# Four transformer blocks on one core: the third bf16 part of queries and keys is copied by POOL's queue instead of SyncE's, and eleven start-up loads are issued at another place

## The chip, the cores and the metric

One core of a Trainium2 chip runs the whole program. The time is device microseconds from launch to end, the median of several runs. The program has the five engines' instruction streams: TensorE (PE), VectorE (DVE), ScalarE (ACT), GpSimd (POOL) and SyncE (SP), each in order. DMAs are started by SP's, ScalarE's and POOL's queues.

## The reference

The input is 16 sequences of 256 tokens with 256 features, and for each a context of 77 tokens. Four layers follow each other:

```python
# layer 0: pre-norm decoder block
x = x + mha(ln1(x), ln1(x), causal) @ m_proj_w + m_proj_b
x = x + mha(ln2(x), ctx)            @ c_proj_w + c_proj_b
x = x + relu(ln3(x) @ f_w1 + f_b1) @ f_w2 + f_b2
# layer 1: post-norm, with a mixture of experts
x = ln1(x + attn(x, x, causal));  x = ln2(x + attn(x, ctx))
p = softmax(x @ router_w + router_b); two best of 8 experts, softmax over the two
x = ln3(x + sum over the two of weight * (gelu(x @ w1[e] + b1[e]) @ w2[e] + b2[e]))
# layer 2: post-norm with a given mask;  layer 3: one more cross attention
x = ln1(x + mha(x, x, mask)); x = ln2(x + mha(x, ctx)); x = ln3(x + relu(x @ w1) @ w2)
x = ln(x + attn(x, ctx) @ Wo)
```

Every attention has 16 heads of 16 features. So there are three self attentions (numbered 0, 2, 4) and four cross attentions (1, 3, 5, 6) per sequence. All data are float32.

## The kernel before

**Three phases.** Phase a runs layer 0 and layer 1 up to the router for all 16 sequences and scatters each token's row to the rows of its two experts. Phase b runs the experts in 39 groups of 256 rows. Phase c gathers the results and runs the rest. The span of the profile divides into a to some 1560 us, b to some 2125 us, and c.

**The plan.** In phases a and c the work of one sequence is a chain of small steps, each on one engine; up to six sequences are in flight. Before anything is emitted, a planner (`Plan.run`) places all steps by costs written beside them (`us`, and `lag` until a result is usable) and gives each engine one fixed list. Among steps that can start at the same time it takes the more urgent one; urgency is the length of the way that is left, plus a lead from the table `AHEAD` (line 437) by stage of the work (`enters`, `norms`, `projs`, `shifts`, `gains`, `outs` and others) and by attention. At run time an engine works through its list in order and waits on semaphores.

**Stacks.** The scores need nearly float32 accuracy from bf16 matmuls. So queries and keys are cut into three bf16 parts: `high` (ScalarE, line 916), `rest` (DVE, 1071), `middle` (ScalarE, 921), `low` (POOL, 1288), in a tile `parts` of 128 partitions. Six blocks of 16 partitions then form a stack (`qs`, `ks`, or `ctx_ks` for the context's keys), in which each part stands once or several times, so that one matmul over 96 rows gives the product. `COPIES` says which: the first part is copied to three blocks, the second to two, the third to one, for each role. Each copy is a DMA from SBUF to SBUF, issued by SP (line 1343), 128 KB, or 38.5 KB for the context's keys. Each part's copies wait for the step that makes the part, and stand in SP's list in the order of the parts. The scores by query (`qm`, line 702, with a mask matmul at 835 or 839) wait for the last copies of both roles.

**Shifts.** DVE takes the maxima of the scores (1081), cuts them in three parts (to line 1100), PE turns them (710), ScalarE copies them to `shift` (925), and SP writes them below the query stack by a DMA (1346). Only then do the scores by key (`km`, 722) and the exponentials (932) follow, then probabilities times values (738), further turns (748, 757) and the output projection (774).

**Other users of the queues.** SP also issues the inputs (1328), the context (1331), the start-up loads (1325) and the stores. POOL does the eps and power steps of the norms (1268, 1273), gains and biases (1280, 1284, 1294), and the indirect scatters and gathers (1308, 1299); in phase b it issues the weights of phase c by plain DMAs (1312).

**Start-up loads.** Groups of constants have a queue and a step behind which they are issued (`LOADS`, line 412). The group `rows` has 14 loads: three bias rows, four gain and shift rows of the norms l1_1 and l1_2, the router and its bias, and five of tables and masks. SP issues them right behind the input of the third sequence.

Of the kernel before, what the change touches and what calls it, by code (L numbers as in the profile page):

```python
# [14 lines left out]
P = 128  # L15
B, S, D = 16, 256, 256
H, HD = 16, 16
# [250 lines left out]
def parts_steps(plan, b, at, role, xt, source, after=(), gives=()):  # L268
# [14 lines left out]
    order = [("copy", b, at, (role, part)) for part in range(NPART)]  # L283
    for part, kind in enumerate(("high", "middle", "low")):
        plan.step("sync", "copy", b, at, (role, part), us=0.63 * len(COPIES[role == "q"][part]), lag={"q": 4.6, "k": 5.6, "c": 2.4}[role],
                  after=[(kind, b, at, role)], behind=order[part - 1:part], gives=["parts"] if part == NPART - 1 else [],
                  landing="stack", transfers=len(COPIES[role == "q"][part]), stack=stack, parts=parts)
    return stack
# [91 lines left out]
def self_attention(plan, b, at, xt, turned):  # L380
# [3 lines left out]
    stacked = [("copy", b, at, (role, part)) for role in "qk" for part in range(NPART)]  # L384
# [3 lines left out]
def cross_attention(plan, b, at, xt, turned, context):  # L388
    qs = parts_steps(plan, b, at, "q", xt, turned, gives=["xt"])
    ks, values = context  # L390
    stacked = [("copy", b, at, (role, part)) for role in "qc" for part in range(NPART)]
# [3 lines left out]
def feed_forward(plan, b, at, xt, turned, residual, with_bias):  # L395
    hidden = ("qs", (b, at))
    for f in range(FT // 2):
# [15 lines left out]
         "bias": ("scalar", None), 1: ("sync", ("enter", 1, "a")), "rows": ("sync", ("enter", 2, "a")),  # L413
# [3 lines left out]
def start_steps(plan, loads):  # L417
    plan.pool("weights", len(LOADS))
    for name, (queue, step) in LOADS.items():
# [5 lines left out]
    plan.step("vector", "fold", -1, "a", us=0.4, after=[("load", -1, "a", "rows")])  # L425
# [11 lines left out]
AHEAD = {"a": {("shifts", 0): 0.1, ("shifts", 1): 2.4, "ends": 0.3, "enters": -1.1, "ffs": 8.0, ("gains", 2): 7.6,  # L437
               "norms": 0.6, ("norms", 3): 3.7, ("norms", "l0_ff"): -0.3, "outs": -0.7, ("outs", 1): 0.3,
               ("outs", 2): 0.6, "projs": 0.8, ("projs", 1): -0.2, "pvs": -1.0, "scores": 0.1, "turns": -0.6,
               ("turns", 1): 3.1, "values": -0.4, ("values", 0): 2.4},  # L440
         "c": {"shifts": 0.8, "ends": 0.1, ("ends", 4): -0.3, "enters": 2.2, "ffs": -0.7, ("ffs", 6): 0.5,
               ("maxima", 5): -0.2, "gains": -4.3, ("norms", 5): 1.2, ("outs", 6): 0.2, "projs": 0.2, "pvs": -0.1,
               "scores": 1.7, ("scores", 6): -0.3, "turns": 0.1, ("turns", 6): 0.1, ("turns", "l2_ff"): -0.4,
# [873 lines left out]
def sync_program(sp, k, phase):  # L1317
# [3 lines left out]
    for s in k.plan.order[phase]["sync"]:  # L1321
# [10 lines left out]
        elif s.kind == "copy":  # L1332
# [5 lines left out]
            elif part == 1:  # L1338
                until.wait_ge(*done("middle", b, at, role))
            else:  # L1340
                until.wait_ge(*done("low", b, at, role))
# [363 lines left out]
```

## Time and profile before

| | us |
|---|---|
| median of 3 runs | 3290.51 (3286.32 to 3300.18) |
| the profiled execution | 3307.31 |
| its span, first to last instruction | 3305.5 |
| PE busy | 3046.6 (92%) |
| DVE busy | 1561.7 (47%) |
| ACT busy | 1541.9 (47%) |
| POOL busy | 872.2 (26%) |
| mean granted clock of PE | 0.960 |

The shares are of the span. DMA issues are not counted as busy on SP's queue, so SP has no row. A wait is put down to what released it. "PEclk" is the granted clock, as a share of full speed. The page counts these stack copies of 128 KB on SP: 384 and 288 for queries, 192 and 96 for keys, in the first and second half, and 192 and 192 of 38.5 KB for the context's keys.

### The profile page before, as it was taken

Reading aid. Unit: us, or ns where it says so; the run is one execution under the profiler, and the core shown is the slowest. Engines: PE = TensorE matmul, PEld = TensorE weight load, DVE = VectorE, ACT = ScalarE, POOL = GpSimd, SP = SyncE. Lnnn points to the kernel's source line nnn. Section 1 sums busy time; section 2 is a strip of 40 time slices with the busy share of each in tenths; the row PEclk is TensorE's granted clock in tenths of the full one; section 3 lists DMA queues with packets and bytes.
Section 4 is the critical chain, followed back from the end, with each engine's and each line's share of the span. In section 5 each row is a group of like instructions: output and inputs, shape, how many; then the busy total and the mean of one; then the engine's idle time right before and its main releaser. Section 6 shows DMA issues by size and latency. Waiting matters only on the chain. (4 is left out here: it accounts for less than half of the span.)

```text
span 3305.5 us, 61810 instructions
## 1 busy us (share of the span) xinstructions
PE 3046.6 (92%) x23959; PEld 2472.7 (75%) x24016; DVE 1561.7 (47%) x4057; ACT 1541.9 (47%) x3403; POOL 872.2 (26%) x991
## 2 busy tenths in 40 slices
PE   7999999899999999885999999789999999999996
PEld 5788877678876777764888888656777777777774
DVE  4644465554466556444101110166555566565542
ACT  3555556455555555452222222145455555555652
POOL 2121234222133322322000000142243444334331
PEclk8999999899999999997999999899999999999997
DMA  9734345463355553743766665365255546444431
GB/s 167 98 53 62 55 69 90 69 91 45 55 78 88 83 74 53 172 62 97 242 218 221 199 198 197 104 107 65 33 73 68 81 69 82 63 71 78 62 49 24
DMA packets 394607, 319.34 MB, mean 97 GB/s; under 512 B 151711, under 2 KB 378271, under 8 KB 394303
## 3 DMA queue, kind: packets, MB, share of 16 engines
q1 hardware_dynamic: 371062, 276.77, 46.8%
q0 software_dynamic: 8272, 23.73, 2.8%
q10 hardware_dynamic: 14981, 14.89, 1.6%
q8 instruction: 190, 3.11, 0.5%
q14 instruction: 102, 0.84, 0.1%
HBM read 134.33 MB, written 37.22 MB: 52 GB/s over the span
## 5 line engine op out<-in xcount | busy, mean ns | idle before, releaser
L1081 DVE TENSOR_REDUCE a_maxima<-a_bank 128x2 f32<-128x512 f32 (+3 forms) x576 | 339.8, 646 | 177.1 <-PE a_bank L702 173.3
L932 ACT ACTIVATE a_prob<-a_bank 128x512 f32<-128x512 f32 (+1 forms) x640 | 338.8, 600 | 138.0 <-PE a_bank L722 134.0
L1081 DVE TENSOR_REDUCE c_maxima<-c_bank 128x2 f32<-128x512 f32 (+2 forms) x448 | 259.1, 636 | 178.5 <-PE c_bank L702 178.3
L932 ACT ACTIVATE c_prob<-c_bank 128x512 f32<-128x512 f32 (+1 forms) x512 | 264.4, 599 | 150.9 <-PE c_bank L722 150.2
L968 ACT ACTIVATE b_group_hidden<-b_bank,b_b 128x256 f32<-128x256 f32 x312 | 131.0, 471 | 421.4 <-PE b_bank L790 421.4
L835 PE MATMUL a_bank<-a_causal_b,keep_identb 128*128 128x256 bf16 (+1 forms) x768 | 248.0, 323 | 57.0 <-DMA a_qs<-a_shift 38.2
L790 PE MATMUL b_bank<-b_group_xt,b_w 128*128 128x256 f32 x1248 | 284.1, 381 | 0.8 <-DVE b_group_xt L1122 0.8
L774 PE MATMUL b_bank<-b_w,b_group_hidden 128*128 128x256 f32 x1248 | 275.8, 379 | 0.9 <-ACT b_group_hidden L968 0.9
L774 PEld LDWEIGHTS b_bank<-b_w,b_group_hidden 128*128 128x128 f32 x1248 | 237.0, 190 | 33.5 <-ACT b_group_hidden L968 1.3
L790 PEld LDWEIGHTS b_bank<-b_group_xt,b_w 128*128 128x128 f32 x1248 | 235.5, 191 | 31.9 <-DVE b_group_xt L1122 1.2
L1127 DVE TENSOR_TENSOR b_group_y<-b_bank,b_b 128x512 f32<-128x512 f32 x39 | 27.0, 691 | 364.4 <-PE b_bank L774 364.4
L1118 DVE TENSOR_TENSOR a_tok<-a_bank,a_tok 128x512 f32<-128x512 f32 x80 | 55.2, 690 | 205.3 <-PE a_bank L774 198.3
L722 PE MATMUL a_bank<-a_qs,a_ks 99*128 99x128 bf16 x1536 | 149.0, 226 | 0.5 <-issue 0.5
L722 PEld LDWEIGHTS a_bank<-a_qs,a_ks 99*128 99x128 bf16 x1536 | 125.6, 102 | 25.0 <-issue 3.8
L702 PE MATMUL a_bank<-a_ks,a_qs 96*128 96x128 bf16 x1536 | 144.0, 223 | 0.0
L943 ACT ACTIVATE a_raw<-a_bank 128x512 f32<-128x512 f32 x128 | 76.4, 597 | 138.7 <-PE a_bank L738 124.7
L702 PEld LDWEIGHTS a_bank<-a_ks,a_qs 96*128 96x128 bf16 x1536 | 122.3, 100 | 24.3 <-issue 2.2
L680 PE MATMUL a_bank<-a_xt,a_at_q 128*128 128x256 f32 x512 | 133.7, 407 | 4.9 <-ACT a_xt L905 2.3
L1288 POOL TENSOR_TENSOR a_parts_q<-a_rest,a_parts_q 128x512 bf16<-128x512 f32 x64 | 74.3, 1160 | 225.3 <-ACT a_parts_q L921 225.2
L774 PE MATMUL a_bank<-a_at_o,a_heads 128*128 128x256 f32 x512 | 128.2, 395 | 5.8 <-ACT a_heads L949 5.7
L835 PEld LDWEIGHTS a_bank<-a_causal_b,keep_identb 128*128 128x128 bf16 x768 | 77.6, 101 | 73.2 <-DMA a_qs<-a_shift 42.0
L1280 POOL TENSOR_TENSOR c_tok<-c_tok,weights_row_L_xattn_ln_g 128x512 f32<-128x512 f32 x64 | 81.6, 1275 | 162.6 <-PE c_bank L671 162.4
(239 smaller groups left out, 6542.4 us busy)
## 6 DMA issues: line engine op xcount, KB each, us to landing
b_w<-in_L_xattn_e_w SPq DMA_DIRECT2D x78, 1024.0 KB, 7.3
a_qs<-a_parts_q SPq DMA_DIRECT2D x384, 128.0 KB
c_qs<-c_parts_q SPq DMA_DIRECT2D x288, 128.0 KB
a_ks<-a_parts_k SPq DMA_DIRECT2D x192, 128.0 KB
c_ks<-c_parts_k SPq DMA_DIRECT2D x96, 128.0 KB
b_group_x<-sorted_in SPq DMA_DIRECT2D x39, 256.0 KB, 6.8
sorted_out<-b_group_y ACTq DMA_DIRECT2D x39, 256.0 KB, 5.2
sorted_in<-a_zeros SPq DMA_DIRECT2D x8, 1024.0 KB
```

What stands on the lines that cost most here:

```text
L680: ins = pe.matmul(bank[:, 0, m * n:(m + 1) * n], weight[:, kt, m * P:(m + 1) * P], xt[:, kt, 0:n], start=(kt == 0), stop=(kt == KT - 1))
L702: ins = pe.matmul(bank[:, 0, to:to + m], qs[0:STACK, h, q * P:(q + 1) * P], ks[0:STACK, h, kt * P:kt * P + m], start=(at in CROSS), stop=( ...
L722: ins = pe.matmul(bank[0:kn, 0, to:to + m], ks[0:STACK + NPART, h, kt * P:kt * P + kn], qs[0:STACK + NPART, h, q0:q0 + m], start=(at in CR ...
L774: ins = pe.matmul(bank[:, 0, q * D:(q + 1) * D], heads[:, kt, q * P:(q + 1) * P], weight[:, kt, :], start=(kt == 0), stop=(kt == kts - 1))
L790: ins = pe.matmul(bank[:, 0, j * S:(j + 1) * S], weight[:, kt, f * P:(f + 1) * P], xt[:, kt, :], start=(kt == 0), stop=(kt == KT - 1))
L835: pe.matmul(blocks, k.identb, k.causal[:, keys_first, :].unsqueeze(1).broadcast_to([P, 4 // step, P]), start=True, stop=False)
L932: act.activation(prob[0:rows, first:first + cols], bank[0:rows, 0, 0:cols], ACT.Exp, scale=SCALE).then_inc(k.own(s), 1)
L943: act.activation(tile(s, "raw"), tile(s, "bank")[:, 0, :], ACT.Copy).then_inc(k.own(s), 1)
L968: ins = act.activation(hidden[:, f, :], bank[:, 0, j * S:(j + 1) * S], ACT.Gelu, bias=b1[:, f:f + 1])
L1081: v.tensor_reduce(maxima[:, q:q + qn, h:h + n].rearrange("p q h -> p h q"), bank[:, 0, 0:cols].rearrange("p (j q n) -> p j q n", j=n, q=qn ...
L1280: pool.tensor_tensor(x, x, over(k.gains[at][0]), ALU.mult).then_inc(k.own(s), 1)
L1288: pool.tensor_tensor(parts[:, 2, :, 0:n], rest[:, :, 0:n], parts[:, 1, :, 0:n], ALU.subtract).then_inc(k.own(s), 1)
```

## The change

The third part's copy becomes a step of POOL, `low_copy`, issued after POOL's own `low` step; SP keeps the copies of the first two parts. PE waits for both. The `high` step, which writes into a `parts` tile, waits for the earlier user's second and third copies. The planner counts 1.0 us of POOL for the new step, where it had 0.63 us of SP, and the same lag. The group `rows` is split: three bias rows stay, and the other eleven loads form the group `gains`, behind the shift DMA of sequence 0's second attention. The table of leads gets other values for both phases, so the order of all engines' lists differs.

```diff
--- before.py
+++ after.py
@@ parts_steps
-    order = [("copy", b, at, (role, part)) for part in range(NPART)]
-    for part, kind in enumerate(("high", "middle", "low")):
-        plan.step("sync", "copy", b, at, (role, part), us=0.63 * len(COPIES[role == "q"][part]), lag={"q": 4.6, "k": 5.6, "c": 2.4}[role],
-                  after=[(kind, b, at, role)], behind=order[part - 1:part], gives=["parts"] if part == NPART - 1 else [],
+    lag = {"q": 4.6, "k": 5.6, "c": 2.4}[role]
+    for part, kind in enumerate(("high", "middle")):
+        plan.step("sync", "copy", b, at, (role, part), us=0.63 * len(COPIES[role == "q"][part]), lag=lag,
+                  after=[(kind, b, at, role)], behind=[("copy", b, at, (role, 0))] if part else [],
                   landing="stack", transfers=len(COPIES[role == "q"][part]), stack=stack, parts=parts)
+    plan.step("gpsimd", "low_copy", b, at, role, us=1.0, lag=lag, after=[("low", b, at, role)],
+              behind=[("copy", b, at, (role, 1))], gives=["parts"], landing="stack", stack=stack, parts=parts)
@@ LOADS
-         "bias": ("scalar", None), 1: ("sync", ("enter", 1, "a")), "rows": ("sync", ("enter", 2, "a")),
+         "bias": ("scalar", None), 1: ("sync", ("enter", 1, "a")), "rows": ("sync", ("enter", 2, "a")), "gains": ("sync", ("shift_in", 0, 1)),
@@ AHEAD
-AHEAD = {"a": {("shifts", 0): 0.1, ("shifts", 1): 2.4, "ends": 0.3, "enters": -1.1, "ffs": 8.0, ("gains", 2): 7.6,
-               "norms": 0.6, ("norms", 3): 3.7, ("norms", "l0_ff"): -0.3, "outs": -0.7, ("outs", 1): 0.3,
-               ("outs", 2): 0.6, "projs": 0.8, ("projs", 1): -0.2, "pvs": -1.0, "scores": 0.1, "turns": -0.6,
-               ("turns", 1): 3.1, "values": -0.4, ("values", 0): 2.4},
-         "c": {"shifts": 0.8, "ends": 0.1, ("ends", 4): -0.3, "enters": 2.2, "ffs": -0.7, ("ffs", 6): 0.5,
-               ("maxima", 5): -0.2, "gains": -4.3, ("norms", 5): 1.2, ("outs", 6): 0.2, "projs": 0.2, "pvs": -0.1,
-               "scores": 1.7, ("scores", 6): -0.3, "turns": 0.1, ("turns", 6): 0.1, ("turns", "l2_ff"): -0.4,
+AHEAD = {"a": {("shifts", 0): 0.1, ("shifts", 1): 2.4, "ends": 0.3, "enters": 1.1, "ffs": 8.0, ("maxima", 0): -0.2,
+               "gains": -0.5, ("gains", 2): 7.6, ("gains", "l0_ff"): -3.9, "norms": 1.2, ("norms", 0): -1.1,
+               ("norms", 3): 3.7, ("norms", "l0_ff"): -0.8, "outs": -0.7, ("outs", 1): 2.2, ("outs", 2): 1.0,
+               "projs": 0.8, ("projs", 1): -0.2, "pvs": -1.0, ("pvs", 1): 0.1, ("pvs", "l0_ff"): -0.2, "scores": 0.1,
+               "turns": -0.6, ("turns", 1): 3.1, "values": -0.3, ("values", 0): 2.4},
+         "c": {"shifts": 0.8, ("shifts", 6): 1.1, "ends": 0.1, ("ends", 4): -0.4, "enters": 0.6, ("enters", 4): -1.0,
+               ("enters", 6): 0.2, "ffs": -0.7, ("ffs", 6): 0.5, ("maxima", 5): -0.2, "gains": -2.1, "norms": -0.1,
+               ("norms", 4): -0.2, ("norms", 5): 1.2, "outs": -0.3, ("outs", 4): -0.3, ("outs", 5): 2.3,
+               ("outs", 6): 0.2, ("outs", "l2_ff"): 3.0, "projs": 0.2, "pvs": -0.1, "scores": 1.7, ("scores", 4): 0.3,
+               ("scores", 5): -0.1, ("scores", 6): -0.3, "turns": 0.1, ("turns", 6): -0.1, ("turns", "l2_ff"): -0.4,
                ("values", 5): 2.0}}
@@ tensor_program, qm
-            until.wait_ge(*done("copy", b, at, ("q", NPART - 1)))
-            until.wait_ge(*done("copy", b, at, ("k" if at in SELF else "c", NPART - 1)))
+            for role in "qk" if at in SELF else "qc":
+                until.wait_ge(*done("copy", b, at, (role, 1)))
+                until.wait_ge(*done("low_copy", b, at, role))
@@ scalar_program, high
-            until.wait_ge(*freed(s, "parts"))
+            earlier = k.plan.earlier[s.tiles["parts"]]
+            if earlier:
+                until.wait_ge(*done(*earlier))
+                until.wait_ge(*done("copy", earlier[1], earlier[2], (earlier[3], 1)))
@@ gpsimd_program
+        elif s.kind == "low_copy":
+            stack, (block,) = tile(s, "stack"), COPIES[s.part == "q"][NPART - 1]
+            until.wait_ge(*done("low", b, at, s.part))
+            until.wait_ge(*freed(s, "stack"))
+            pool.dma_start(stack[block * HD:(block + 1) * HD, :, :],
+                           tile(s, "parts")[:, NPART - 1, :, 0:C if s.part == "c" else S]).then_inc(k.own(s), 16)
@@ sync_program, copy
-            elif part == 1:
+            else:
                 until.wait_ge(*done("middle", b, at, role))
-            else:
-                until.wait_ge(*done("low", b, at, role))
...
```

The steps that waited for the load `rows` and need one of the moved constants (the fold of a bias into a shift row, the router's matmul, the table steps) wait for `gains` instead.

## Rows read from the trace of the kernel before

**Rows 1.** The page: the engines' busy us and shares; DVE's maxima, mean ns of one.

```profile
PE 3046.6 (92%) x23959; PEld 2472.7 (75%) x24016; DVE 1561.7 (47%) x4057; ACT 1541.9 (47%) x3403; POOL 872.2 (26%) x991
...
L1081 DVE TENSOR_REDUCE a_maxima<-a_bank 128x2 f32<-128x512 f32 (+3 forms) x576 | 339.8, 646 | 177.1 <-PE a_bank L702 173.3
```

**Rows 2.** Windows: us; busy us (count) of PE, PEld, DVE, ACT, POOL; PEclk, DMA share, GB/s.

```profile
100.00:1400.00 1300.00, 1219.06 (x11265) 1002.23 (x11263) 712.37 (x1959) 695.55 (x1523) 358.37 (x403) 0.97 0.51 76
...
1400.00:1562.00 162.00, 103.97 (x994) 82.15 (x994) 70.91 (x226) 64.21 (x134) 40.74 (x44) 0.81 0.37 74
...
2181.00:3200.00 1019.00, 986.44 (x7847) 759.65 (x7902) 608.30 (x1471) 563.76 (x1242) 362.93 (x407) 0.99 0.48 67
...
3200.00:3306.00 106.00, 73.29 (x468) 54.15 (x466) 32.80 (x94) 32.03 (x70) 23.83 (x28) 0.78 0.18 31
```

**Rows 3.** Waits of PE: line, releaser, us in total, times, longest.

```profile
PE a_bank L835 <- DMA a_qs<-a_shift: 38.2, 12, 9.1
...
PE c_bank L722 <- DMA c_qs<-c_shift: 29.8, 13, 7.2
...
PE a_bank L722 <- DMA a_qs<-a_shift: 7.2, 3, 3.7
...
PE a_bank L835 <- DMA a_qs<-a_parts_q: 6.0, 3, 4.2
```

**Rows 4.** Windows around the wait of PE at 600 us.

```profile
590.00:608.00 18.00, 8.19 (x83) 6.87 (x82) 13.59 (x42) 5.42 (x13) 6.04 (x5) 0.79 1.12 142
608.00:615.00 7.00, 7.00 (x56) 5.70 (x57) 0.00 (x0) 3.78 (x7) 0.00 (x0) 0.57 0.16 22
```

**Rows 5.** The chain that ended last, at 2873 and 3273: start, us, what.

```profile
2873.61 7.96 DMA c_qs<-c_shift
...
3273.19 2.72 DMA c_qs<-c_shift
```

**Rows 6.** Timeline of SP's queue and ScalarE before that shift: start, us, what.

```profile
2872.31 0.61 SPq L1343 DMA_DIRECT2D c_ks<-c_parts_k  x1
...
2872.96 0.61 SPq L1343 DMA_DIRECT2D c_qs<-c_parts_q  x1
...
2873.61 0.75 SPq L1346 DMA_DIRECT2D c_qs<-c_shift  x1
...
2872.79 0.38 ACT L925 ACTIVATE c_shift<-c_bank 48x256 bf16<-48x256 f32 x1 [1.37 <-PE c_bank L710]
```

**Rows 7.** Window of the burst ahead of it.

```profile
2868.00:2875.00 7.00, 7.00 (x63) 5.53 (x57) 5.88 (x14) 5.10 (x13) 4.56 (x6) 1.00 1.14 124
```

**Rows 8.** Groups of POOL's DMAs: count, busy us, mean ns, idle before.

```profile
L1308 POOL DMA_INDIRECT sorted_in<-a_tok,keep_rows x64 | 63.8, 997 | 87.4 <-DVE keep_rows L1206 65.1 <-issue 15.5 <-DMA x_moe_in<-a_tok 6.9
...
L1312 POOL DMA_DIRECT2D weights_row_L_xattn_ln_g<-in_rows x4 | 2.2, 545 | 54.4 <-DMA b_group_x<-sorted_in 54.4
...
L1312 POOL DMA_DIRECT2D c_weights_at_v<-in_L_xattn_ca_wv x1 | 0.7, 712 | 13.4 <-DMA b_group_x<-sorted_in 13.4
```

**Rows 9.** Lines 1308 and 1312 (last row): duration ns and landing, min/median/max.

```profile
L1308 POOL DMA_INDIRECT sorted_in<-a_tok,keep_rows x64: 959/963/1227, 473.5 to 1547.3; - x64
...
DMA to landing us min/median/max: 6.4/7.5/8.8
...
DMA to landing us min/median/max: 3.2/3.4/9.2
```

**Rows 10.** Timeline of SP's queue and PE at the start.

```profile
16.41 0.43 SPq L1325 DMA_DIRECT2D a_row_L_xattn_ln_g<-in_rows  x1
...
21.39 1.97 SPq L1343 DMA_DIRECT2D a_ks<-a_parts_k  x3
...
34.80 0.59 PE L835 MATMUL a_bank<-a_causal_b,keep_identb 128*128 128x512 bf16 x1 [4.18 <-DMA a_qs<-a_parts_q]
```

**Rows 11.** Waits of SP's queue for POOL, the largest.

```profile
SPq L1343 <- POOL c_parts_q L1288: 18.2, 11, 2.0
```

**Rows 12.** Timeline of PE: the first scores that read the stack of rows 6.

```profile
2885.34 0.38 PE L702 MATMUL c_bank<-c_ks,c_qs 96*128 96x256 bf16 x2
```

More of the change, by code:

```diff
@@ L383, in self_attention @@
     values = value_steps(plan, b, at, "v", xt, turned, after=[("proj", b, at, "k")], gives=["xt"])
-    stacked = [("copy", b, at, (role, part)) for role in "qk" for part in range(NPART)]
+    stacked = [(kind, b, at, part) for role in "qk" for kind, part in (("copy", (role, 1)), ("low_copy", role))]
     return attend_steps(plan, b, at, qs, ks, values, stacked)
@@ L390, in cross_attention @@
     ks, values = context
-    stacked = [("copy", b, at, (role, part)) for role in "qc" for part in range(NPART)]
+    stacked = [(kind, b, at, part) for role in "qc" for kind, part in (("copy", (role, 1)), ("low_copy", role))]
     return attend_steps(plan, b, at, qs, ks, values, stacked)
@@ L424, in start_steps @@
     plan.step("vector", "cast", -1, "a", us=1.0, after=[("load", -1, "a", "first"), ("load", -1, "a", "masks")])
-    plan.step("vector", "fold", -1, "a", us=0.4, after=[("load", -1, "a", "rows")])
+    plan.step("vector", "fold", -1, "a", us=0.4, after=[("load", -1, "a", "gains")])
 STAGES = {"enters": ("enter", "ctx_load"), "norms": ("stats", "moments", "eps", "rstd", "apply"), "turns": ("turn", "turned"),
@@ L507, in route_steps @@
     r = ("route", b)
-    plan.step("tensor", "route", b, "a", us=0.86, source=turned, after=[("load", -1, "a", "rows")], takes=["bank", "r"], gives=["xt"],
+    plan.step("tensor", "route", b, "a", us=0.86, source=turned, after=[("load", -1, "a", "gains")], takes=["bank", "r"], gives=["xt"],
               xt=xt, bank=bank, r=r)
@@ L814, in tensor_program @@
             xt = tile(s, "xt")
-            until.wait_ge(*done("load", -1, "a", "rows"))
+            until.wait_ge(*done("load", -1, "a", "gains"))
             until.wait_ge(*done(*s.source))
@@ L1006, in vector_program @@
         elif s.kind == "fold":
-            until.wait_ge(*(done("load", -1, "a", "rows") if at == "a" else k.c_loaded))
+            until.wait_ge(*(done("load", -1, "a", "gains") if at == "a" else k.c_loaded))
             for shift, bias in k.folds[at]:
@@ L1222, in table_step @@
     until.wait_ge(*(k.done("table", s.b, "a", s.part - 1) if s.part else k.done("run", s.b, "a")))
-    until.wait_ge(*k.done("load", -1, "a", "rows"))
+    until.wait_ge(*k.done("load", -1, "a", "gains"))
     if s.part == 0:
@@ L1539, in build_phases @@
         k.out_bias["l0_ff"] = row(c, n0("f_b2"))
+        c.group = "gains"
         k.gains["l1_1"], k.gains["l1_2"] = [(row(c, n1(f"ln{i}_g")), row(c, n1(f"ln{i}_b"))) for i in (1, 2)]
@@ L1567, in build_phases @@
                             (k.run[:, 0, :], a["regions"].partition_broadcast(P))]
-        c.loads["rows"] += [(k.table["steps"], a["steps"].partition_broadcast(P)),
+        c.loads["gains"] += [(k.table["steps"], a["steps"].partition_broadcast(P)),
                             (k.table["upto"].rearrange("p a b -> p (a b)"), a["upto"].partition_broadcast(1)),
```

## The prediction

> **What bounds the kernel now.** I read four views, in this order. The page gives TensorE (PE) 92% of the span [rows 1], so the first question is what the other 8% is and not which engine to relieve. The windows by stage [rows 2] place it. From 100 to 1400 us (first half, steady) PE is busy 1219 of 1300 us: 81 us idle, and its granted clock averages 0.97. While the first half drains (1400 to 1562) it is busy 104 of 162 us. In the steady second half 986 of 1019, in its tail 73 of 106. The expert stage between them runs full and has no step of this change. So the second half can give some 33 us steady and 33 in the tail, and the first half 81 and 58, plus what the clock loses.
>
> The waits of PE by releaser [rows 3] say who ends that idle time. The largest releaser in either half is a DMA that SP's queue issued: the row shifts into the query stack (38.2, 7.2 and 29.8 us) and, small, the query parts into the stack (6.0). Together 81.2 us in 31 waits. A long one costs more than its length: after the wait of 7.7 us at 600 the clock is 0.57 over the next 7 us, the lower of its two levels (1.2 of 2.4 GHz) for most of it, 3.0 us of work lost [rows 4].
>
> The fourth view is the chain around one such wait. The shift DMA issued at 2873.61 is the longest link, 7.96 us, where one with nothing in front of it takes 2.72 us at 3273.19 [rows 5]. ScalarE had the shift ready at 2872.79 + 0.38 = 2873.17; SP still issued two third parts, 0.61 us each, so 0.44 us went by in SP's queue [rows 6]. The other 7.96 - 2.72 = 5.2 us are spent behind earlier transfers: 16 DMA engines are 1.14 busy from 2868 to 2875 and move 124 GB/s [rows 7], or 128 KB in 1.06 us, while SP issues one each 0.65 us. So in a burst the transfers, more than the issuing, set when the shift lands.
>
> **The change part by part.** *Copies moved.* One copy per role and attention: per sequence 8 in the first half, 6 in the second, times 16 = 224 of 1344; 64 of them are of the short context keys. SP loses 224 x 0.61 = 137 us of issuing, spread over 2700 us. Most of it buys nothing, as SP sits idle between bursts. It counts where a shift DMA stands behind them. SP's waits for POOL's low step vanish too: the largest group is 18.2 us in 11 [rows 11], and the queued copies behind it (those of the next part or the shift) become free.
>
> What one wait gains, from both sides: nothing, if the shared engines are the limit; at most two issues (1.2 us) plus one sixth of the 5.2 us backlog (0.9), if the third parts leave the ring that the shift queues in and are served in the gaps: 2.1 us. At the row read closely only 0.4 of the issue time was usable, and I give half of the ring's share, because POOL's copies want the same engines at the same time: 0.4 + 0.5 = 0.9 us. Without the start's wait (below) 30 waits are left, so 27 us. Clock: the long wait has 3.0 us lost beside 7.7, short ones nothing at 0.99 mean [rows 2, 4]; I take a factor 1.2, which is 32 us. PE's order is fixed, so part of it is handed to the next wait; no other releaser comes near in total, so I keep two thirds: **-21 us** (bounds 0 and 30 x 2.1 x 1.4 = -88).
>
> The Trainium skill (DMA: Bandwidth & Descriptors, Issuing engines are not separate DMA queues) says that DMAs of several issuing engines end up on the same 16 engines and that spreading the issue saves only the issuer's time. The 1.14 busy share of [rows 7] agrees. By that rule alone the 0.5 us of ring share is nothing, and the term would be 30 x 0.4 x 1.2 x 2/3 = -10 us. It is the second rival below.
>
> *POOL's added work.* The trace has no stack copy from POOL. The nearest are its direct loads: 0.54 us for 128 KB of rows and 0.71 for 256 KB of weights; an indirect one takes 1.00 us, with some 0.3 us between two [rows 8]. I price the 160 long copies as the former and the 64 short as the latter, plus 0.3 each: 86 + 46 + 67 = 199 us (upper bound by the indirect rows, 224 x 1.3 = 290; lower bound without gaps 132). POOL goes from 363 busy of 1019 us in the second half [rows 2] to some 450. What stands behind a copy on POOL: the eps and rstd steps of the norms, gains, biases, gathers and scatters. A norm step meets an issue in some 8% of cases (199 us of 2700), for half an issue, and PE then waits for DVE's apply step; over 160 norms that is 160 x 0.08 x 0.45 = 6 us on a chain that is mostly hidden under five other sequences. **+2 us** (0 to +8). If that cover were gone it would be the 6 us, twice in places where POOL also has gathers.
>
> *Landing of the third part.* The scores start only with every part in place. On SP the last third part was issued at 2872.96 and the scores that read it began at 2885.34 [rows 6, 12], 12.4 us later. POOL's direct loads land 3.4 us after the issue in the median, 9.2 at worst, its scatters 7.5 [rows 9]. Even 9.2 plus two 1.3 us elementwise steps ahead of it fits into 12.4. Cost 0 where the slack is like this; rival three prices where it isn't. The `high` step's wait for a free parts buffer now names both copies; the same events, no cost.
>
> *An issue held up by DVE.* 64 scatters, issued on POOL beside a DVE that is busy over half of the time [rows 2], take 959/963/1227 ns at the least, middle and most [rows 9]: held up by 0.27 us at most. Cost 0; rival four is the other case. The Trainium skill (SBUF — State Buffer, the trap "DVE blocks DMA") says that DVE instructions in certain modes keep GpSimd from writing the descriptors of its DMAs, 620 ns becoming 3100; the trace disagrees so far.
>
> *The constants.* Fourteen loads are issued behind the third sequence's input at the start. By the diff three stay (`rows`) and eleven (`gains`) go behind a shift DMA of sequence 0's second attention. Eleven issues stand from 16.41 to 21.39, 5.0 us, and the first copy into a stack comes right after, at 21.39; PE's first scores wait 4.18 us for those copies and start at 34.80 [rows 10]. With the copies 5 us earlier this wait goes: **-4 us** (0 to -6; sequence fill has later waits that can take it back). The eleven come back as 5 us of SP's queue in the middle of sequence 0's copies, once: **+2 us** (0 to +5).
>
> *The order.* The planner's leads are changed for 13 entries and more, enters, norms, outs, gains above all, in both halves; every engine's list comes out different. No row prices that. The 81 idle us of 100 to 1400 are single waits with no period, so a new order deals them anew: 0, with +-15.
>
> Sum: -21 + 2 - 4 + 2 = -21 us. The profiled execution took 3307.31 us (span 3305.5); with the change 3286. It is 16.8 us above the median of the timed runs, 3290.5; the same step from there gives **3269.5 us**, -0.64%.
>
> **The rivals.** *One, the new order is itself better.* Leads that fit the queues close waits that no copy causes, a third of the steady 81 + 33 us and of the clock's 39 (1300 x 0.03): some 50 us, 3240. For it: the large first-half waits are irregular. Against: it needs most of them to close together.
>
> *Two, it hides anyway.* The DMA engines set the landing, SP's freed time is idle time; the start gives 2 to 4 and the rest is noise: 3290.5 - 3 = 3287. For it: [rows 7], and that the landing stays at 8 us however the copies are split. Against: [rows 6] has the shift behind two of the very copies that move.
>
> *Three, the third part becomes the late one.* It waits in POOL's order behind elementwise steps, then needs 7.5 us like a scatter instead of some 3.4. Its place is the first scores matmul of an attention; it decides from where less than about 10 us lie between issue and scores. If that is so for one in four of the 112 attentions, with 1.3 us each and the clock's 1.2: 28 x 1.3 x 1.2 = 44 us, less 9 of what the forecast gains: 3325. For it: query parts already end three waits of PE [rows 3]; waits of POOL's own kind at the drain, where nothing covers. Against: the slack of 12.4 us.
>
> *Four, DVE holds up POOL's issues.* An issue that has to wait for a DVE instruction of 0.65 us, the mean of its maxima [rows 1], costs up to that each time: 224 x 0.65 = 146 us more on POOL, which then issues for 345 us; a norm step meets that in 13% of cases for 0.8 us, 160 x 0.13 x 0.8 = 17 us, and with third parts 0.65 us later the forecast's gain is gone beside it: -21 + 17 + 2 = 3288. Against: the scatters' 0.27 us. The skill's SBUF rule above is this rival.
>
> **How the numbers follow.** Forecast 0.42; rival one 0.12; two 0.25; three 0.18; four 0.03. About 0.5% (16 us) is what a measurement tells from no change, so faster means under 3274. The forecast with its +-15 falls there for 0.36 of its 0.42 when its size is right, but its size is uncertain by half, so 0.31; rival one gives 0.12, rival two 0.05: faster 0.48. Slower (over 3307): 0.17 from three, 0.03 from two, 0.01 from the forecast: 0.21. Same 0.31. Range: rival one and most of three inside, 3230 to 3315.
>
> **What would show it.** Right: PE's waits for the two shift DMAs fall from 75 to about 50 us in sum; the first scores start near 30.6 instead of 34.80; POOL-issued stack copies at 0.5 to 0.7 us; mean clock of 100 to 1400 rises. Wrong: the shift's link stays near 8 us (rival two), PE waits for `low_copy` transfers by name (rival three), or issues on POOL over 1.3 us (the rule on DVE).

## The result, and the profile after

The changed kernel takes **3342.51 us** (median of 4 runs, 3332.84 to 3345.05); the kernel before, measured beside it, 3289.94 (4 runs, 3286.32 to 3300.18). The ratio is **1.0148** (95% interval 1.0123 to 1.0174): 1.5% slower, where 0.64% faster was forecast. The profiled executions took 3345.05 and 3307.31 us.

The page after, first part and DMA queues (packets, MB, share of 16 engines):

```profile
PE 3051.1 (91%) x23951; PEld 2479.2 (74%) x24016; DVE 1554.1 (46%) x4057; ACT 1547.6 (46%) x3403; POOL 1008.4 (30%) x1215
...
q1 hardware_dynamic: 330614, 253.26, 42.5%
q0 software_dynamic: 18000, 47.24, 8.0%
```

The queues before:

```profile
q1 hardware_dynamic: 371062, 276.77, 46.8%
q0 software_dynamic: 8272, 23.73, 2.8%
```

TensorE does the same work. POOL has 1008.4 - 872.2 = 136 us more, the moved copies and no more. Their 23.5 MB have gone from q1 to q0. The two queues together take 50.5% of the engines' time where they took 49.6%; in e1 below, with the same order and every copy on SP, they take 50.6%, so the larger share need not come from the issuer (columns as above):

```profile
q1 hardware_dynamic: 371062, 276.77, 47.8%
q0 software_dynamic: 8272, 23.73, 2.8%
```

The windows that answer to [rows 2], and PE's waits that answer to [rows 3]:

```profile
100.00:1400.00 1300.00, 1209.39 (x11271) 1000.58 (x11268) 711.85 (x1960) 696.66 (x1521) 422.85 (x512) 0.97 0.54 78
1400.00:1562.00 162.00, 110.33 (x1009) 87.54 (x1010) 69.11 (x222) 65.84 (x138) 43.95 (x50) 0.79 0.35 84
2181.00:3200.00 1019.00, 956.31 (x7503) 734.31 (x7564) 579.06 (x1415) 544.10 (x1193) 393.99 (x467) 0.97 0.47 63
```

```profile
PE c_bank L728 <- DMA c_qs<-c_shift: 58.7, 12, 7.2
PE a_bank L841 <- DMA a_qs<-a_shift: 58.2, 14, 18.8
PE a_bank L728 <- DMA a_qs<-a_shift: 12.8, 7, 3.8
...
PE a_bank L841 <- DMA a_ks<-a_parts_k: 6.1, 2, 5.2
...
PE a_bank L708 <- DMA a_ctx_ks<-a_parts_k: 2.3, 2, 1.2
PE a_bank L841 <- DMA a_qs<-a_parts_q: 1.8, 1, 1.8
```

Lines 841, 728 and 708 are 835, 722 and 702 of before. In the steady second half PE is busy for 30 us less (986.44 to 956.31), and its clock is two hundredths lower; its wait for the shift has doubled (29.8 to 58.7). The same releaser as before ends these waits, so no new wait appeared: the old one grew. The next table divides the time by phase. A half ends with PE's last instruction of it; the second half is counted from the end of the expert phase, which takes some 561 us in each. "Low clock" is the time at which PE's granted clock stood at 1.2 GHz and not 2.4.

| profile | first scores at | first half ends | second half lasts | low clock in the second half |
|---|---|---|---|---|
| before | 34.8 | 1542.3 | 1172.0 | 92.6 |
| before, a second profile | 35.2 | 1540.1 | 1171.3 | 89.0 |
| after | 31.8 | 1530.5 | 1218.8 | 157.0 |

**All of the loss is in the second half: +47 us.** The first half of this trace ends 10 to 12 us earlier, but two other kernels with the same first half (below) end it at 1542.6 and 1547.2, so that is no gain to rely on. Of the 47 us, PE's idle time makes up 28.5 (82.3 to 110.8 in the second half), which is the growth of the one wait for the shift (28.9). The low clock lasted 64 us longer, and at half speed that costs 32. Together this is 14 us more than the loss; what gave those back is open.

The chain of waits after, its links of this kind in the second half (start, us, what; "..." marks rows left out):

```profile
2748.31 8.59 DMA c_qs<-c_shift
...
2821.81 9.68 DMA c_qs<-c_shift
2831.54 2.78 PE c_bank L728 x12
...
2895.33 8.29 DMA c_qs<-c_shift
...
2967.35 9.83 DMA c_qs<-c_shift
...
3309.36 2.74 DMA c_qs<-c_shift
```

Against [rows 5] the link behind a burst of copies has grown, from 7.96 us to between 8.3 and 9.8; the one with nothing ahead of it has not. It recurs once per sequence. SP's queue around it shows what changed (first after, then the row of before that follows the shift of [rows 6]):

```profile
2878.90 6.42 SPq L1356 DMA_DIRECT2D c_qs<-c_parts_q  x8
2885.37 3.22 SPq L1356 DMA_DIRECT2D c_ks<-c_parts_k  x5
2888.63 1.26 SPq L1356 DMA_DIRECT2D c_qs<-c_parts_q  x2
2890.37 4.27 SPq L1356 DMA_DIRECT2D c_ctx_ks<-c_parts_k  x5
2895.33 0.76 SPq L1359 DMA_DIRECT2D c_qs<-c_shift  x1
```

```profile
2874.46 4.84 SPq L1343 DMA_DIRECT2D c_ctx_ks<-c_parts_k  x6
```

Before, the context's key copies of the next attention stood behind the shift of attention 5. After, five of them stand ahead of it, though SP has fewer copies in all: the planner has put them there.

PE and the clock around the wait at 2825 us, and the windows over it (columns as in [rows 2]):

```profile
2823.76 1.89 PE L796 MATMUL c_bank<-c_xt,c_weights_f 128*128 128x256 f32 x8
2831.54 2.78 PE L728 MATMUL c_bank<-c_qs,c_ctx_ks 99*77 99x256 bf16 x12 [5.89 <-DMA c_qs<-c_shift]
```

```profile
2824.00:2832.00 8.00, 2.11 (x11) 1.53 (x10) 0.00 (x0) 2.41 (x6) 2.18 (x2) 0.87 0.77 50
2832.00:2836.00 4.00, 3.78 (x17) 2.83 (x17) 0.69 (x1) 3.12 (x6) 0.00 (x0) 0.50 0.00 0
```

After 5.9 us without work PE runs at least 4 us at half clock.

### The profile page after: what moved, and what is told of

Read it like the earlier page. It is cut to its first block and busy times, and to the rows that moved or that the text cites. A ratio compares the mean times of both kernels' runs of the same rounds, so it can differ in the third digit from the quotient of the medians.

```text
span 3343.1 us, 62041 instructions
## 1 busy us (share of the span) xinstructions
PE 3051.1 (91%) x23951; PEld 2479.2 (74%) x24016; DVE 1554.1 (46%) x4057; ACT 1547.6 (46%) x3403; POOL 1008.4 (30%) x1215
## 5 line engine op out<-in xcount | busy, mean ns | idle before, releaser
L1090 DVE TENSOR_REDUCE a_maxima<-a_bank 128x2 f32<-128x512 f32 (+2 forms) x576 | 339.2, 647 | 140.2 <-PE a_bank L708 139.6
L841 PE MATMUL a_bank<-a_causal_b,keep_identb 128*128 128x256 bf16 (+1 forms) x768 | 245.5, 320 | 73.4 <-DMA a_qs<-a_shift 58.2
L728 PE MATMUL c_bank<-c_qs,c_ctx_ks 99*77 99x256 bf16 x512 | 85.8, 315 | 61.0 <-DMA c_qs<-c_shift 58.7
L1297 POOL TENSOR_TENSOR c_parts_q<-c_rest,c_parts_q 128x512 bf16<-128x512 f32 x48 | 55.6, 1158 | 255.4 <-ACT c_parts_q L930 255.4
L685 PE MATMUL a_bank<-a_xt,a_at_q 128*128 128x256 f32 x512 | 127.0, 392 | 4.4 <-ACT a_xt L911 2.3
```

The costliest lines, as they stand in the source:

```text
L685: ins = pe.matmul(bank[:, 0, m * n:(m + 1) * n], weight[:, kt, m * P:(m + 1) * P], xt[:, kt, 0:n], start=(kt == 0), stop=(kt == KT - 1))
L728: ins = pe.matmul(bank[0:kn, 0, to:to + m], ks[0:STACK + NPART, h, kt * P:kt * P + kn], qs[0:STACK + NPART, h, q0:q0 + m], start=(at in CR ...
L841: pe.matmul(blocks, k.identb, k.causal[:, keys_first, :].unsqueeze(1).broadcast_to([P, 4 // step, P]), start=True, stop=False)
L1090: v.tensor_reduce(maxima[:, q:q + qn, h:h + n].rearrange("p q h -> p h q"), bank[:, 0, 0:cols].rearrange("p (j q n) -> p j q n", j=n, q=qn ...
L1297: pool.tensor_tensor(parts[:, 2, :, 0:n], rest[:, :, 0:n], parts[:, 1, :, 0:n], ALU.subtract).then_inc(k.own(s), 1)
```

## The experiments

Between 2300 and 3200 us PE waits for the shift of attention 5 once per sequence, ten times in most kernels (the count is given where it differs). Each such wait divides exactly. *Queue* is the time from the shift being ready on ScalarE to the issue of its DMA. *Issue to go* runs from that issue to the first scores by key. *PE work* is what PE still had to do once the shift was ready. Then queue + issue to go - PE work = wait. The table gives means per wait, the sum of all of them, and how long the second half lasts, in us.

| kernel | queue | issue to go | PE work | wait | sum of waits | second half |
|---|---|---|---|---|---|---|
| before | 0.62 | 7.48 | 6.34 | 1.76 | 17.6 | 1172.0 |
| after | 0.29 | 9.27 | 4.73 | 4.82 | 48.2 | 1218.8 |
| e1, SP issues all | 1.72 | 8.30 | 4.73 | 5.29 | 52.9 | 1223.7 |
| e2, POOL issues, old lists (9 waits) | 0.02 | 7.93 | 6.37 | 1.59 | 14.3 | 1179.0 |
| e3, old leads in the second half (6) | 0.47 | 9.15 | 5.30 | 4.32 | 25.9 | 1222.5 |
| e4, before, shift on ScalarE (9) | 0.03 | 7.69 | 6.28 | 1.44 | 12.9 | 1162.3 |
| e5, after, shift on ScalarE | 0.03 | 9.58 | 4.77 | 4.84 | 48.4 | 1220.0 |
| f1, after, shift first | 0.03 | 7.54 | 4.73 | 2.83 | 28.3 | 1189.4 |
| f4, before, context first | 4.26 | 5.99 | 6.33 | 3.92 | 39.2 | 1207.9 |
| g2, before, new leads | 0.67 | 8.36 | 5.11 | 3.92 | 39.2 | 1217.1 |

The expectations name four theories. R: third copies on POOL's queue hold up the shift. O: the new leads leave PE too little work between a shift and the scores by key. Neither outlived e1 to e3, and P and L took their place. P: the planner puts copies ahead of the shift in SP's list. L: what matters is PE's own list. All ratios are to the kernel before on the same chip (median 3312 to 3319 there, 22 to 29 us above that of the main comparison), with the 95% interval. "..." in a diff marks lines left out.

**Third copies back on SP, everything else as after** (each third copy is put into SP's list at its planned time):

```diff
+        began = lambda s: self.began[s.kind, s.b, s.at, s.part]
+        order["sync"] = sorted(order["sync"] + [s for s in order["gpsimd"] if s.kind == "low_copy"], key=began)
+        order["gpsimd"] = [s for s in order["gpsimd"] if s.kind != "low_copy"]
...
```

> The changed kernel with the lists of PE, DVE, ACT and POOL as they are, but the third copies issued by SP, at the time where the planner put them; POOL only loses them. Theory R (the third copies on POOL's ring hold up the shift DMA and make the second half slower): the wait of PE for the c_qs shift, 58.7 us in the changed kernel, falls back to about 30 us and the time to about 3290 to 3300 us. Theory O (the new leads' order of the second half leaves too little PE work between a shift and the scores by key): the wait stays at 50 to 75 us and the time at 3335 to 3355 us.

Measured: 3357.59 us, 1.0134 (1.0107 to 1.0161), as slow as the changed kernel: theory R fails.

```profile
PE c_bank L733 <- DMA c_qs<-c_shift: 63.8, 13, 7.2
```

Who issues the third parts matters little in the second half (1223.7 us against 1218.8); the lists do.

**Third copies on POOL, the lists of before** (each right behind its `low` step):

```diff
+            third = {(s.b, s.at, s.part[0]): s for s in order["sync"] if s.kind == "copy" and s.part[1] == NPART - 1}
+            order["sync"] = [s for s in order["sync"] if not (s.kind == "copy" and s.part[1] == NPART - 1)]
+            order["gpsimd"] = [x for s in order["gpsimd"] for x in
+                               ([s, third[s.b, s.at, s.part]] if s.kind == "low" else [s])]
...
```

> The kernel before with all its lists, but the third copies issued by POOL, each right behind the low step. Theory R: the second half grows by about 50 us as in the changed kernel, the time is 3330 to 3345 us. Theory O: the copies' mover is harmless or a small gain, 3275 to 3300 us, the wait for the c_qs shift 20 to 35 us.

Measured: 3331.55, 1.0053 (1.0034 to 1.0072); first half to 1557.9, second half 1179.0. The time lies in R's range, but not for R's reason: that was to be some 50 us in the second half, which grew by 7, and the wait for the shift is as O had it.

```profile
PE c_bank L729 <- DMA c_qs<-c_shift: 26.5, 12, 8.1
PE c_bank L677 <- DVE c_tok L1073: 17.3, 11, 4.9
```

The move alone costs 0.5%, a third of the loss, and most of that in the first half. It shortens the queue term from 0.62 to 0.02 us, lengthens issue to go by 0.45, and leaves the wait about where it was. The second row is PE's wait for DVE's step of a norm, which itself stands behind POOL's eps and power steps. It was 7.4 us in 3 waits before (10.7 in the second profile of that kernel): part of what the move costs in the second half goes through the norms.

**After, with the old leads in the second half** (the `"c"` table of `AHEAD` from before):

> The changed kernel with the leads of the kernel before in the second half only (first half and POOL's copies as changed). Theory O: the second half goes back to its 1172 us or some 10 more, and with the first half 12 us shorter as in the changed kernel's profile the time is 3275 to 3295 us. Theory R: the second half stays at 1210 to 1225 us, the time at 3330 to 3350 us.

Measured: 3356.49, 1.0116 (1.0073 to 1.0159); second half 1222.5, against O's 1172 to 1182. Theory O fails: the old leads do not bring the time back once the planner charges the third copy to POOL.

```profile
PE c_bank L726 <- DMA c_qs<-c_shift: 39.0, 9, 7.1
...
PE c_bank L714 <- DVE c_least_parts L1107: 10.5, 5, 2.7
...
PE c_bank L706 <- DMA c_ks<-c_parts_k: 9.2, 2, 7.9
```

The shift waits are not the whole story here. They grew by 9 us (29.8 to 39.0), while all idle time of PE in the second half grew by 32 (82.3 to 114.2). The rest is spread over others: the last piece of the maxima (the L714 row; 2.6 us before), a key copy, DVE's norm step (14.3, 7.4 before).

**Before, with the new leads** (both tables of `AHEAD` from after, all copies on SP):

> The kernel before with the changed kernel's two tables of leads, third copies on SP and counted there. By the lists that come out, in 6 sequences of the second half the shift DMA of attention 5 has no context copy in the run of copies ahead of it, in others 3 to 6. If it is the leads that put the context copies ahead of the shift, the second half is 1210 to 1225 us; if it takes the planner's counting of the third copies on POOL as well, it is 1170 to 1195 us, the time 0.998 to 1.008 of the kernel before.

Measured: 3372.5, 1.0178 (1.0155 to 1.0201); second half 1217.1, first half to 1560.0.

```profile
PE c_bank L725 <- DMA c_qs<-c_shift: 49.6, 12, 7.2
```

The new leads alone, with no copy on POOL and no load moved, cost as much as the whole change in the second half (+45 us), and 18 us more in the first. In the six last of the ten sequences no context copy stands in the burst ahead of the shift. The wait grows through less PE work between the shift and the scores by key (6.34 to 5.11) and a later landing (7.48 to 8.36). So context copies ahead of the shift are one way to lose this time, and not the only one: e3 and g2 each have one half of the new plan, and each loses as much as both halves together.

**Before, context copies ahead of the shift.** Nothing else is altered: in 8 sequences the six copies of attention 6's context keys change places with the shift of attention 5.

```diff
+            line = order["sync"]
+            for i in range(len(line) - 1, -1, -1):
+                s = line[i]
+                if s.kind == "shift_in" and s.at == 5:
+                    j = i
+                    while j + 1 < len(line) and line[j + 1].kind == "copy" and line[j + 1].at == 6 and line[j + 1].part[0] == "c":
+                        line[j], line[j + 1] = line[j + 1], line[j]
+                        j += 1
```

> The kernel before with the reverse: in SP's list of the second half the six context-key copies of attention 6 that stand behind the shift DMA of attention 5 (8 sequences) stand ahead of it. Theory P: each of the 8 shifts lands about 2.5 us later, or with SP's 6 x 0.65 us of issuing up to 4; PE's wait for the c_qs shift rises from 30 to 50 to 60 us, the second half by 20 to 45 us; the time is 1.006 to 1.014 of the kernel before. Theory L: within 0.3% of the kernel before.

Measured: 3354.79, 1.0128 (1.0104 to 1.0153); second half +36 us, as P expected.

```profile
PE c_bank L731 <- DMA c_qs<-c_shift: 49.7, 12, 7.2
```

```profile
2892.21 5.05 SPq L1352 DMA_DIRECT2D c_ctx_ks<-c_parts_k  x6
2897.30 0.75 SPq L1355 DMA_DIRECT2D c_qs<-c_shift  x1
```

Six small copies in front of the shift reproduce most of the loss. They do it by another term than in the changed kernel, though: here SP's queue grows (0.62 to 4.26 us) and issue to go shrinks (7.48 to 5.99), while in the changed kernel SP has issued the copies before the shift is ready, and issue to go grows (to 9.27).

**After, the shift ahead of those copies** (11 sequences), the opposite edit:

```diff
+            line = order["sync"]
+            for i, s in enumerate(line):
+                if s.kind == "shift_in" and s.at == 5:
+                    j = i
+                    while line[j - 1].kind == "copy" and line[j - 1].at == 6 and line[j - 1].part[0] == "c":
+                        line[j], line[j - 1] = line[j - 1], line[j]
+                        j -= 1
```

> The changed kernel with one change in SP's list of the second half: where the shift DMA of attention 5 stands behind context-key copies of attention 6 (one to five transfers, 11 sequences), it now stands ahead of them. Nothing else moves. Theory P (the planner, which counts a copy at its issuing queue only, filled the time freed on SP with those copies ahead of the shift, and it lands about 2.5 us later): PE's wait for the c_qs shift falls from 58.7 to 25 to 40 us, and with the lower clock behind waits of 4 to 6 us the second half gets 20 to 40 us shorter; the time is 0.6 to 1.2% below the changed kernel, so 1.003 to 1.009 of the kernel before. Theory L (it is the work that PE has between the shift and the scores, set by PE's list): the wait stays over 50 us, the time within 0.3% of the changed kernel's.

Measured: 3327.63, 1.0036 (1.0023 to 1.0050), as P expected and not L; second half 1189.4, 29 us of the 47 recovered.

```profile
PE c_bank L736 <- DMA c_qs<-c_shift: 38.7, 12, 7.2
```

Issue to go returns to that of before (9.27 to 7.54). The missing PE work (4.73) stays, and so does a wait 1.1 us longer than before; this is the likely, untested, cause of the 17 us that are left of the loss.

**The shift issued by ScalarE**, right behind the instruction that makes it, in before:

```diff
+            shifts = {(s.b, s.at): s for s in order["sync"] if s.kind == "shift_in"}
+            order["sync"] = [s for s in order["sync"] if s.kind != "shift_in"]
+            order["scalar"] = [x for s in order["scalar"] for x in
+                               ([s, shifts[s.b, s.at]] if s.kind == "turned_shift" else [s])]
...
```

> The kernel before, with the shift DMA issued from ScalarE's queue right behind the step that makes the shift, not from SP's; everything else, lists included, as before. If the backlog of SP's ring is what makes a shift land after 8 us and not 2.7, it lands after 3 to 5 us, most of PE's 75 us of waits for it go, and the time is 3240 to 3265 us. If the 16 shared engines set the landing whatever the ring, it stays near 8 us and the time at 3285 to 3295 us.

Measured: **3265.11, 0.9855 (0.9827 to 0.9884)**; first half to 1510.4, second half 1162.3.

```profile
PE c_bank L727 <- DMA c_qs<-c_shift: 21.8, 12, 5.0
PE a_bank L840 <- DMA a_qs<-a_shift: 15.8, 5, 5.8
PE a_bank L727 <- DMA a_qs<-a_shift: 2.8, 2, 1.9
```

and the same edit in after:

> The changed kernel with the shift DMA issued from ScalarE's queue, right behind the step that makes it. It no longer stands behind SP's copies and the clearing DMAs (18.8 us wait at 1385 us), but shares the 16 engines with all that was issued before. Theory P: most of what the change lost comes back, since what stands ahead in SP's list no longer matters for the issue: about 0.988 to 0.998 of the kernel before, as the same step took 1.45% from the kernel before. If the loss is in PE's list, 1.003 to 1.010 is left.

Measured: 3315.8, 1.0011 (0.9996 to 1.0027); first half to 1504.8, second half still 1220.0. P had expected 0.988 to 0.998 and misses; the result lies between that and the 1.003 to 1.010 of a loss in PE's list. The copies ahead of the shift delay it whichever queue issues it.

```profile
PE c_bank L733 <- DMA c_qs<-c_shift: 56.6, 12, 5.9
```

The own queue takes away the whole queue term and nothing of issue to go, which is 7.69 us in e4 (7.48 before) and 9.58 in e5 (9.27 after). So e4's expectation came out by halves: the landing as if the shared engines set it, the time as if it had become short. Most of the gain, 32 of the 40 us by which e4's trace is shorter, is in the first half, where SP's queue held some shifts back for long. In the changed kernel one shift was ready at 1380.49 and could go only behind this row of clearing stores,

```profile
1369.39 23.46 SPq L1369 DMA_DIRECT2D sorted_in<-a_zeros  x9
```

which gave PE its longest wait for a shift, 18.8 us (9.1 in before, [rows 3]). The Trainium skill (DMA: Bandwidth & Descriptors, Issuing engines are not separate DMA queues) says that DMAs started by several engines run on the same 16 DMA engines, and that spreading the issue saves only the issuer's time. Both runs agree: issue to go did not shorten.

**Two refinements of e4.** First, SP waits in the second half, at the shift's old place, until the shift is made, so that no copy passes it (sync_program):

```diff
         elif s.kind == "shift_in":
             until.wait_ge(*done("turned_shift", b, at))
-            sp.dma_start(tile(s, "qs")[STACK:STACK + NPART, :, :], tile(s, "shift")).then_inc(k.own(s), 16)
...
```

> The kernel before with the shift DMA issued by ScalarE as in e4, but in the second half SP waits at the old place of the shift until the shift is made, so that the context copies behind it don't come earlier. If the backlog of the shared engines at the moment of the issue sets the landing, the shifts land sooner than in e4 (7.4 us where PE waited) by up to 2 us and the second half is 1150 to 1160 us against e4's 1162; if the copies that follow don't matter, it stays at 1160 to 1168 us.

Measured: 3261.59, 0.9844 (0.9822 to 0.9867); second half 1164.3, no shorter than e4's 1162.3, so the copies that follow don't matter. Second, e4 with the eleven constants loaded later:

> Two steps on the kernel before together: the shift DMA on ScalarE's queue in both halves (1.45% alone) and the eleven loads later. If both gains add up: 0.983 to 0.986 of the kernel before.

Measured: 3265.05, 0.9844 (0.9826 to 0.9861). e4, g3 and g4 beat the kernel before by the same 1.5%, and the changed kernel, 1.5% slower than it, by some 3%; their intervals don't part them.

**Before, only the eleven loads later**, behind the same shift DMA as in after. DVE's step that folds one of them moves with them; the lists are otherwise unchanged:

```diff
+            late = [s for s in line if s.kind == "load" and s.part == "gains"]
+            line = [s for s in line if s not in late]
+            i = [(s.kind, s.b, s.at) for s in line].index(("shift_in", 0, 1)) + 1
+            order["sync"] = line[:i] + late + line[i:]
...
```

> The kernel before with all its lists, but the eleven loads of gains, router and tables issued behind the shift DMA of sequence 0's second attention, and the DVE step that folds one of them moved to just before it is needed. The prediction's term: first scores 3 to 5 us earlier than in the kernel before on the same kind of chip (34.8 to 35.2 us in the two profiles), the end of the first half 0 to 5 us earlier: 0.998 to 1.000. The rival, that later waits of the fill take it back: first scores earlier, end of the first half unchanged within 3 us.

Measured: 3312.88, 0.9982 (0.9969 to 0.9994), 2 to 10 us faster. First scores at 33.2, 1.6 to 2.0 us earlier than in the two profiles of before, where 3 to 5 were expected; the first half of this one trace ends later (1546.1), so the trace does not show where the gain lies.

**The kernel before, profiled once more:**

> The kernel before, unchanged, for a second profile on this chip, to compare the others with. 1.000, waits for the shifts within 10 us of those of the first profile.

Measured: 3303.98 in one execution. Its second half (1171.3), its wait per shift (1.83) and its first half (1540.1) show how far two profiles of one kernel differ: little.

## Why the prediction was wrong, point by point

**The failed step is the term for the order, "0, with +-15".** The text had said that every engine's list comes out different and that no row prices that, and then took zero because the *first half's* idle time is irregular. The second half is not like that: one shift wait recurs in each sequence, the chain passes through it [rows 5], and PE was already waiting there, 1.2 to 2.3 us each time. So no slack was left: whatever delays the shift, or takes PE's work from under it, is paid once per sequence. Measured: +47 us in the second half (after), +45 by the new leads alone (g2), +36 by one exchange in SP's list (f4). That f1 gives back 29 of the 47 shows the exchange to be the larger part of this change's own loss; 17 us remain with the 1.6 us less of PE work after the shift is ready (6.34 to 4.73), which no run restored by itself. That part is measured in the table; that it is the cause is only argued. The parts also do not add up: the leads alone lose 45 us, and the planner's new charge with the old leads 50 (e3). Why any change of this plan costs some 45 to 50 us, and whether the old leads had been fitted to the old plan, no run tested.

The clock was mis-sized beside it. The text had short waits cost nothing; here the longer ones recurred, and 64 us more at the low clock cost about as much as the waiting itself.

Why the planner did so can be read in its costs. It charges a copy to the queue that issues it and gives the shift a fixed lag (2.2 us, times 1.35, behind 0.76 of issuing), where the traces have 7.5 to 9.3; the 16 shared engines are in neither. With third copies off SP the plan has room in SP's list, and fills it ahead of the shift. This is a reading of the code; no run charged the planner for the shared engines to test it. On the chip the engines are as full as before: 20 transfers of SP (five of them short) and four of POOL go ahead of the shift at 2895, where 18 went ahead of the one at 2873.

**The copies moved, -21 us: worth nothing.** PE's waits for the shifts were to fall from 75 to about 50 us; they rose to 58.7 + 58.2 + 12.8 = 130. On unchanged lists (e2) they fell only from 75.2 to 36.5 + 9.4 + 26.5 = 72.4, and the two halves of the reasoning can be seen apart: the queue share did go (0.60 us, forecast 0.4), but the ring share didn't (issue to go 0.45 *longer*, forecast 0.5 shorter). So the term was worth about 3 us of waits and nothing of the time. The Trainium skill (DMA: Bandwidth & Descriptors, Issuing engines are not separate DMA queues) says that issuing from more engines saves only the issuer's time, and by it the ring share is nothing. The trace of e2 agrees; the forecast had named the rule and given half of the share against it.

**POOL's added work, +2 us: priced right, hidden wrong.** The busy time rose by 136 us, against 132 for the copies without gaps; single issues take 0.53 to 0.81 us with 0.3 between. But e2 pays 17 us (0.53%) for the move, beyond the bound of 8. In its second half PE's wait for DVE's norm step rose by 7 to 10 us, the very path that the term had called mostly hidden. What carries the 16 us of the first half was not tested.

**Third part's landing, 0: right.** The landing took 2.8/6.5/12.9 us (least, median, most), nearer to the scatters' 7.5 than to the plain loads' 3.4 in the median, and the slack held: PE waited for such a copy by name 2.3 us in 2 waits. Rival three fails. The row that says so:

```profile
  PE a_bank L708: 2.3, 2
  ACT a_parts_k L925: 1.7, 1
busy tenths in 40 slices 0000000000000000000000000000000000000000
DMA to landing us min/median/max: 2.8/6.5/12.9
```

**An issue held up by DVE, 0: right.** The durations of POOL's issues (min/median/max ns):

```profile
L1308 POOL DMA_DIRECT2D a_qs<-a_parts_q x64: 530/584/740, 20.6 to 1480.9; - x64
...
L1308 POOL DMA_DIRECT2D a_ctx_ks<-a_parts_k x32: 643/694/756, 27.6 to 1442.8; - x32
```

None comes near the 1.3 us that was to show it. The longest of the 224 took 0.81 us. The trap "DVE blocks DMA" of the Trainium skill (SBUF — State Buffer) is not seen in them; whether a DVE instruction of the kind that it names ran beside one of them, no run here shows. Rival four fails.

**The constants, -4 + 2: right in sign and size, with luck in the sign that was to show it.** g1 gives -2 to -10 us for the edit by itself. The first scores came at 31.8 instead of 34.80 (30.6 forecast), but this trace is the earliest of its kind: the four other kernels made from the changed one have them at 34.0 to 35.8, and g1 at 33.2. Those with the start-up loads of before have them at 34.8 to 38.1.

**Rivals one and two.** The new order was to be better with a chance of 0.12. No rival had it worse, though the term's own +-15 spoke for both signs alike; 0.01 of slower was all that the forecast left for it. That is where the 1.5% lay, and why the range (to 3315) missed it. Rival two was right on the mechanism that it names, and its 3287 assumed the order harmless too. Of the other signs that were to show the forecast right, POOL's issues came as said and the mean clock of 100 to 1400 us did not rise (0.97 in both).

## What to carry to other kernels

Where a planner writes the order, a change of its costs or leads is a change of every queue: compare the lists around the transfer that recurs on the chain, count what stands ahead of it, and do not price "the order" at zero. For such a wait write down its four parts (queue, landing, other work, wait). Where the wait is there in every period, no slack is left, and each us of delay costs at least itself: here 3 us of waiting cost 5. A late small transfer on a crowded queue was helped here by another engine's queue, which took away the queue term but not the engines' backlog.

## What the runs showed of the hardware

- **The clock fell behind the longer waits of PE.** All traces together have 134 waits of PE for the shift between 2300 and 3200 us. Behind each of the 56 of 3.1 us and more the granted clock stood at 1.2 GHz for a part of the next 8 us, behind none of the 36 under 1.8 us. Between 1.8 and 2.8 us it fell in 15 of 42, not ordered by length: behind one of 1.84 us (g3), not behind one of 2.74 (f1). Time at the low level from 2300 to 3200: 13.7 us before, 68.3 after. So 3 us more of waiting per sequence cost 5: eight periods took 68.2 us each before and 73.3 after.
- **Whether the third copies load the DMA engines more from POOL's queue is open.** On the lists of after, the two queues took 50.6% of the engines' time with these copies on SP (e1) and 50.5% with them on POOL; on the lists of before, 49.6% and 50.3% (e2).
- **Landing depends on the load, not on the issuer**: issue to go for the same shift is 7.5 us behind the burst of before and 9.3 behind the fuller one of after, and from ScalarE's queue 7.7 and 9.6; alone it lands after 2.7.
